# Sixteen-head local attention in f32: the product with V taken in two rounds of 64-row tiles, root steps kept in PSUM, and a new table of places

## The reference

```
for i in range(6):
    x = attn_layer(shift_tokens(x), Wqkv[i], q_scale[i], k_scale[i], Wo[i]) + x
    x = ffn_layer(shift_tokens(x), ln_g[i], ln_b[i], W1[i], b1[i], W2[i], b2[i]) + x

# attn_layer: 16 heads of 64; q, k normalised per head, rotated (rotary tables)
# local_attention, windows of w = 32 tokens:
bk2, bv2 = look(bk), look(bv)                 # window before, own window
sim = einsum('bhwie,bhwje->bhwij', bq, bk2) * 8
sim = where(mask, -max, sim)                  # of the 64 keys: 0 <= i - j <= 32
attn = softmax(sim, -1)
out = einsum('bhwij,bhwje->bhwie', attn, bv2)

# every normalisation: (x - mean) / sqrt(var + 1e-5)
```

## Time and profile before

| | before |
|---|---|
| median of 3 runs | 3553.56 us (3552.68 to 3554.56) |
| profiled execution, first to last instruction | 3553.3 us |
| TensorE matmul busy | 3325.9 us (94%) |
| VectorE busy | 2737.3 us (77%) |
| ScalarE busy | 2545.5 us (72%) |
| GpSimd busy | 2041.5 us (57%) |
| bytes moved by DMA | 423.34 MB, 119 GB/s |

### The profile page before, as it was taken

How to read it: one execution, slowest core, us unless ns; L and a number is a source line. 1 busy time by engine, 2 the same in 40 slices (tenths; PEclk the granted TensorE clock), 3 DMA queues, 4 the chain that set the end, 5 groups by cost and what they waited for, 6 DMA issues and landing times.

```text
span 3553.3 us, 149054 instructions
## 1 busy us (share of the span) xinstructions
PE 3325.9 (94%) x65032; PEld 2107.6 (59%) x65032; DVE 2737.3 (77%) x3420; ACT 2545.5 (72%) x5866; POOL 2041.5 (57%) x1557
## 2 busy tenths in 40 slices
PE   7999987999999999999999999999999999999996
PEld 3444434666666666666666666666666666666663
DVE  3656557888887878888788878788888878788883
ACT  4667655777777777777777767677777777787774
POOL 0000006766676666766666666667676667676661
PEclk9999998999999999999999999999999999999998
DMA  3223224333333333433333333334333333333330
GB/s 109 76 71 84 75 61 141 135 127 127 134 133 133 118 127 130 140 131 129 119 122 136 130 124 127 127 124 143 126 130 126 121 136 125 135 127 131 129 122 24
DMA packets 247337, 423.34 MB, mean 119 GB/s; under 512 B 71966, under 2 KB 110108, under 8 KB 246556
## 3 DMA queue, kind: packets, MB, share of 16 engines
q1 hardware_dynamic: 220368, 397.28, 33.1%
q10 hardware_dynamic: 26316, 16.52, 1.6%
HBM read 124.21 MB, written 7.34 MB: 37 GB/s over the span
## 4 chain that ended last, share of the span: by engine, by line
PE 64%; DVE 17%; issue 7%; ACT 5%; POOL 5%; DMA 1%; SPq 1%; DVEq 0%; POOLq 0%; ACTq 0%
PE PS L535 64%; DVE TPB L932 5%; DVE MX L956 2%; ACT SC L1237 1%; DVE NV L947 1%; POOL K L1324 1%; POOL Q L1342 1%; DMA RB<-root_scratch 1%; POOL K L1342 1%; DVE PP L977 1%; DVE PX L978 1%; DVE NV L945 1%; DVE H L800 1%; DVE H L1000 1%; DVE NV L949 1%
## 5 line engine op out<-in xcount | busy, mean ns | idle before, releaser
L932 DVE SCALAR_TENSOR_TENSOR TPB<-PS,VEC,C 128x1024 f32<-128x1024 f32 x768 | 961.8, 1270 | 102.0 <-ACT SX L1213 95.0
L1237 ACT ACTIVATE SC<-PS,BQ,RQ 128x64 f32<-128x64 f32 x3072 | 979.5, 436 | 40.7 <-DVE BQ L961 40.3
L1213 ACT ACTIVATE SX<-PS 128x512 f32<-128x512 f32 x768 | 461.5, 620 | 391.4 <-PE PS L535 388.4
L1324 POOL TENSOR_TENSOR K<-K,RB 128x512 f32<-128x512 f32 x384 | 497.2, 1295 | 283.1 <-DMA RB<-root_scratch 278.4
L1347 POOL TENSOR_TENSOR SC<-SC,RC 128x1024 f32<-128x1024 f32 x192 | 366.3, 1908 | 480.2 <-DVE RC L969 478.8
L535 PEld LDWEIGHTS PS<-PP,VV 32*64 32x64 f32 x24576 | 433.7, 133 | 278.6 <-issue 276.3
L535 PE MATMUL PS<-PP,VV 32*64 32x64 f32 (+1 forms) x24576 | 541.2, 223 | 7.8 <-issue 6.2
L1342 POOL TENSOR_TENSOR K<-TPB,TR 128x512 f32<-128x512 f32 x384 | 496.4, 1293 | 0.0
L1342 POOL TENSOR_TENSOR Q<-TPB,TR 128x512 f32<-128x512 f32 x384 | 495.5, 1290 | 0.0
L535 PE MATMUL PS<-LXH,LH 128*128 128x512 f32 x768 | 371.3, 484 | 85.2 <-DVE TPB L932 68.4
L535 PE MATMUL PS<-K,Q 64*32 64x64 f32 (+1 forms) x24576 | 302.2, 224 | 49.5 <-issue 48.0
(11 more groups left out here) (167 smaller groups left out, 5809.8 us busy)
## 6 DMA issues: line engine op xcount, KB each, us to landing
TR<-TPB SPq DMA_DIRECT2D x768, 256.0 KB, 2.7
RB<-root_scratch SPq DMA_DIRECT2D x768, 128.0 KB
PP<-PX SPq DMA_DIRECT2D x192, 192.0 KB, 2.6
WS<-in_wqkv ACTq DMA_DIRECT2D x72, 128.0 KB, 2.4
PP<-PX SPq DMA_DIRECT2D x192, 48.0 KB, 2.5
QA<-TH SPq DMA_DIRECT2D x128, 64.0 KB, 2.1
QA<-TL SPq DMA_DIRECT2D x128, 64.0 KB, 2.1
KA<-TH SPq DMA_DIRECT2D x128, 64.0 KB, 2.1
```

What stands on the lines that cost most here:

```text
L932: e.scalar_tensor_tensor(TPB[:, n % 3:4 + n % 2:3 + n % 2 - n % 3, w, :], g, VEC[:, l, 9 + w:10 + w], C[:, at:at + 1024].rearrange("p (o c ...
L1213: e.activation(SX[i % 3][:, :], bk("PJ", key)[:, :], ACT.Square).then_inc(sem["pj_act"], 1)
L1237: p = e.activation(SC[m % 2][:, g, :, :].rearrange("p x k -> p (x k)"), bank[s][:, at:at + 64], ACT.Exp, bias=BQ[m % 2][:, g:g + 1], scale ...
L1324: e.tensor_tensor(dst, dst, RB[n % 2][:, :], ALU.mult).then_inc(sem["pr_pool"], 1)
```

## The change

1. **PV in two rounds.** The keys of two windows stand together in one tile of K = 64 rows. Their queries span three windows, so the moving operand has 96 columns, and `PP` gets three blocks instead of two; where a key window is not used by a query window, the block is zero. A round still has 16 matmuls.
2. **Where the probabilities come from.** Both transposes write to staging tiles (`PX[0]`, `PX[1]`), and eight DMAs of 32 partitions carry them to their blocks. GpSimd zeroes `PP` once.
3. **Root steps in PSUM.** `rsqrt` writes its first two steps back into the bank, the third one too for F2, and F3 reads the bank. `FX` and `EZ` are gone. The F2 bank is now held until F3 is done, and the banks of the other normalisations until the third step.
4. **A new `PLACE`.** Nearly all numbers move a little. ScalarE has two table loads a unit, as before.

```diff
-    o.put("N2", kind, b, banks=[(None, kind + "_root", 3, 1)])
-    o.keep(o.bank["N2", (kind, b), 0], kind + "_root", 3 * b + 1)
+    o.put("N2", kind, b, banks=[(None, kind + "_root", 3, 3)])
+    o.keep(o.bank["N2", (kind, b), 0], kind + "_root", 3 * b + 3)
...
-        lay(z + P["F2"], group, "F2", u, "f2_dve", 3 * u + 1)
+        lay(z + P["F2"], group, "F2", u, "f3_dve", u + 1)
...
-                        on.wait_ge("pv_pe", 4 * m - 4)
-                    on.wait_ge("tt_dve", 2 * m + 2)
-                    e.dma_start(z[0:96, 1, :, :], a[32:128, :, :]).then_inc(sem[f"px_in{m % 2}"], 16)
-                    e.dma_start(z[96:128, 1, :, :].rearrange("p (x c) a -> p x c a", c=4)[:, :, 0:3, :],
-                                a[0:32, :, :].rearrange("p (x c) a -> p x c a", c=4)[:, :, 1:4, :]).then_inc(sem[f"px_in{m % 2}"], 16)
+                        on.wait_ge("pv_pe", 2 * m - 2)
+                    on.wait_ge("tt_dve", 2 * m + 1)
+                    for r in range(4):
+                        k = slice(32 * r, 32 * r + 32)
+                        e.dma_start(z[k, r % 2, :, :], PX[0][k, :, :]).then_inc(sem[f"px_in{m % 2}"], 16)
+                    on.wait_ge("tt_dve", 2 * m + 2)
+                    for r in range(1, 4):
+                        e.dma_start(z[32 * r - 32:32 * r, 1 + (r + 1) % 2, :, :],
+                                    PX[1][32 * r:32 * r + 32, :, :]).then_inc(sem[f"px_in{m % 2}"], 16)
+                    e.dma_start(z[96:128, 2, :, :].rearrange("p (x c) a -> p x c a", c=4)[:, :, 0:3, :],
+                                PX[1][0:32, :, :].rearrange("p (x c) a -> p x c a", c=4)[:, :, 1:4, :]).then_inc(sem[f"px_in{m % 2}"], 16)
...
                     for c in range(4):
-                        for x in range(2):
+                        for t in range(2):
                             for s in range(2):
-                                r = (rho + 2 * x + s) % 4
-                                j = 4 * c + r
-                                w = min(2, 16 - j)
+                                x = (t + rho) % 2
+                                j = 4 * c + 2 * t
+                                w = min(3, 16 - j)
                                 h = 2 * ((2 * p + x) % 8) + s
-                                y = mm(bank[2 + x][64 * s:64 * s + 64, 32 * j:32 * j + 32 * w],
-                                       VV[32 * r:32 * r + 32, c, 64 * h:64 * h + 64],
-                                       PP[p % 2][32 * r:32 * r + 32, 0:w, 8 * s + 4 * x + c, :],
-                                       rho == 0 and c == 0, rho == 3 and c == 3, skip_group_check=True)
+                                k = slice(64 * t, 64 * t + 64)
+                                y = mm(bank[2 + x][64 * s:64 * s + 64, 32 * j:32 * j + 32 * w], VV[k, c, 64 * h:64 * h + 64],
+                                       PP[p % 2][k, 0:w, 8 * s + 4 * x + c, :], rho == 0 and c == 0, rho == 1 and c == 3,
+                                       skip_group_check=True)
...
-            def rsqrt(v, u, x, step, done, r):
+            def rsqrt(v, x, y, step, done, r):
                 on.wait_ge(step, 2 * r + 2)
-                e.scalar_tensor_tensor(u, v, EPS, x, ALU.add, ALU.mult).then_inc(sem[done], 1)
+                e.scalar_tensor_tensor(v, v, EPS, x, ALU.add, ALU.mult).then_inc(sem[done], 1)
                 on.wait_ge(done, 3 * r + 1)
-                e.scalar_tensor_tensor(u, u, -0.5, x, ALU.mult, ALU.mult).then_inc(sem[done], 1)
+                e.scalar_tensor_tensor(v, v, -0.5, x, ALU.mult, ALU.mult).then_inc(sem[done], 1)
                 on.wait_ge(done, 3 * r + 2)
-                e.scalar_tensor_tensor(x, u, 1.5, x, ALU.add, ALU.mult).then_inc(sem[done], 1)
+                e.scalar_tensor_tensor(y, v, 1.5, x, ALU.add, ALU.mult).then_inc(sem[done], 1)
...
-                        on.wait_ge("pv_pe", 4 * m - 4)
                     on.wait_ge("np_pool", m + 1)
-                    e.transpose(PP[m % 2][:, 0, :, :], SC[m % 2][:, :, 1, :]).then_inc(sem["tt_dve"], 1)
-                    e.transpose(PX[:, :, :], SC[m % 2][:, :, 0, :]).then_inc(sem["tt_dve"], 1)
+                    e.transpose(PX[0][:, :, :], SC[m % 2][:, :, 1, :]).then_inc(sem["tt_dve"], 1)
+                    e.transpose(PX[1][:, :, :], SC[m % 2][:, :, 0, :]).then_inc(sem["tt_dve"], 1)
...
-                    rsqrt(bk("F2", key)[:, :], H[0][:, :], FX[:, :], "f2_act", "f2_dve", u)
+                    rsqrt(bk("F2", key)[:, :], H[0][:, :], bk("F2", key)[:, :], "f2_act", "f2_dve", u)
...
-                    e.tensor_tensor(H[2][:, :], H[1][:, :], FX[:, :], ALU.mult).then_inc(sem["f3_dve"], 1)
+                    e.tensor_tensor(H[2][:, :], H[1][:, :], bk("F2", key)[:, :], ALU.mult).then_inc(sem["f3_dve"], 1)
```

Of `PLACE`, the rows that the prediction speaks of:

```diff
-    ... "PV": (4.410, 5.233, 5.448, 5.789) ... "F2n": 14.625, "F3": 15.347 ... "NM2": -3.290, "RW": -3.234 ...
+    ... "PV": (4.497, 5.187) ... "F2n": 14.659, "F3": 14.692 ... "NM2": -3.084, "RW": -2.988 ...
```

More of the change, by code:

```diff
@@ L29 @@
 PLACE = {
[13 rows of a table removed]
[8 rows of a table added]
+    "AQd": -0.504, "AV": (-11.356, 0.560), "AVa": -0.483, "AS": -1.210, "ASa": -1.531, "ASd": -1.446, "AY": 0.834,
+    "AE": 2.282, "AEa": 3.137, "AR": (13.916, 25.437), "AI": (24.693, 25.209, 27.040), "AM": (28.617, 0.665),
+    "AMd": -0.785, "AO": (30.518, 0.702), "NM": (36.012, 37.027, 36.826), "AZ": 39.366,
+    "NX": (43.184, 43.848, 44.893), "AW": 47.832,
 }
@@ L294, in order @@
                 lay(n + P["S3"][i], o.put, "S3", m, i)
+            for i in range(2):
                 lay(n + P["PV"][i], o.put, "PV", m, i)
@@ L379, in build @@
         ES = sb("ES", [128, L])
-        EZ = sb("EZ", [128, L])
         SC = [sb(f"SC{i}", [128, 16, 2, 32]) for i in range(2)]
-        PP = [sb(f"PP{i}", [128, 2, 16, 32]) for i in range(2)]
-        PX = sb("PX", [128, 16, 32])
+        PP = [sb(f"PP{i}", [128, 3, 16, 32]) for i in range(2)]
+        PX = [sb(f"PX{i}", [128, 16, 32]) for i in range(2)]
         XCH = sb("XCH", [128, L], F32R)
@@ L427, in nroot @@
         def nroot(kind):
-            return EZ if kind == "end" else NZ[("in", "mid", "x").index(kind)]
+            return ES if kind == "end" else NZ[("in", "mid", "x").index(kind)]
         def nused(kind, b):
@@ L730, in tensor_program @@
                         on.wait_ge("vp_act", 8 * u + 4 * half + 4)
-                        on.wait_ge(f"px_in{p % 2}", 32 * (p // 2) + 32)
-                        on.wait_ge("tt_dve", 2 * p + 1)
+                        on.wait_ge(f"px_in{p % 2}", 128 * (p // 2) + 128)
                         if p:
@@ L832, in vector_program @@
                     kind, b = key
-                    rsqrt(bk("N2", key)[:, :], nsq(kind)[:, :], nroot(kind)[:, :], kind + "_log", kind + "_root", b)
+                    rsqrt(bk("N2", key)[:, :], nroot(kind)[:, :], nroot(kind)[:, :], kind + "_log", kind + "_root", b)
                 elif st == "AX":
@@ L1224, in scalar_program @@
                     if u:
-                        on.wait_ge("pv_pe", 16 * u - 8 + 8 * hf)
+                        on.wait_ge("pv_pe", 8 * u - 4 + 4 * hf)
                     on.wait_ge("vp_pe", j + 1)
@@ L1248, in scalar_program @@
                         on.wait_ge("wo_pe", p // 4)
-                    on.wait_ge("pv_pe", 4 * p + 4)
+                    on.wait_ge("pv_pe", 2 * p + 2)
                     e.copy(AOT[:, 2 * p % 8:2 * p % 8 + 2, :], PS[:, 2:4, :]).then_inc(sem["pv_act"], 1)
@@ L1263, in scalar_program @@
                     on.wait_ge("f2_pe", u + 1)
-                    ln_exp(H[0][:, :], bk(st, key)[:, :], FX[:, :], -0.5, "f2_act", u + 1, cn("hilo")[:, 3:4])
+                    ln_exp(H[0][:, :], bk(st, key)[:, :], H[0][:, :], -0.5, "f2_act", u + 1, cn("hilo")[:, 3:4])
                 elif st == "F4g":
@@ L1344, in gpsimd_program @@
                     m, = key
+                    if m == 0:
+                        for z in PP:
+                            e.memset(z[:, :, :, :], 0.0).then_inc(sem["band_pool"], 1)
                     on.wait_ge("su_dve", 2 * m + 2)
```

10 lines of the change are left out of this document (5 added, 5 removed), and 21 rows, old and new, of the table PLACE.

## The result

| | before | after |
|---|---|---|
| median | 3554.06 us (3552.68 to 3556.06) | 3614.09 us (3612.39 to 3616.03) |
| ratio, 95% interval | | 1.0171 [1.0156, 1.0185] |
| span of the profiled execution | 3553.3 us | 3613.1 us |
| granted clock over the span | 0.984 | 0.961 |
| bytes moved by DMA | 423.34 MB | 472.24 MB |

The change makes the kernel 60 us slower. The forecast was 3383 us with 0.93 for faster: wrong in sign, and 144 us above the top of the range.

What follows compares the result with a forecast made beforehand. TensorE was taken as the bound for some 70 to 77% of its busy time, VectorE for most of the rest. The sum was 3553.3 - 170 (rounds) - 12 (root steps) - 12 (stalls) + 24 (F2 bank) = 3383 us, range 3310 to 3470.

Steps and rivals of the forecast that it cites:

- the turn without queueing loads: TensorE's changed PV rounds: a turn takes 0.086 us, near its stream, bounds 0.080 and 0.113.
- TensorE's saving: PV in two rounds instead of four saves TensorE 1.14 us a pair, 219 us over 192 pairs.
- the stalls without a cause: TensorE's idle "issue" time, 44.4 us in the stretch: falls 19% with fewer records, 12 us gained.
- The rivals on loads: TensorE's PV rounds: loads queue within a row group (3446 us, chance 0.12) or never overlap its products (3662 us, 0.04).
- The prediction's sign of being wrong: GpSimd's wait for the norm roots' read-back well above its earlier share, TensorE waiting ahead of the scores; or rounds above 1.26 us.
- The table costed at nothing: New PLACE numbers: the shifted places leave the sequence around the costed points as it was, at no cost.
- the cover of 3.2 us: Time from GpSimd's end at 2050.30 to the scores' start at 2053.51, taken to hide roots' writes 2.0 us later.
- the case (3450 to 3550 us): Rival: SyncE's fuller queue and the F2 bank take the gain back, 3549 us at the worst; chance 0.08.
- The F2 bank term: TensorE's V projection waits for F3 on the held bank: 0.5 us a unit lost, 24 us, bounds 0 and 94.
- The share that reaches the end: Part of TensorE's 219 us that shortens the kernel: 0.775, products plus issue on the chain, giving 170 us.
- The rival in which all of it arrives: VectorE doesn't take over, so everything TensorE saves reaches the end: 3300 to 3330 us, chance 0.14.
- Root steps in PSUM: VectorE's three root steps take 646 ns each: 0.50 us a unit, 24 us, half on the chain, 12 gained.

Runs made afterwards that it cites:

- e4: Kernel before, with F2's root steps in PSUM, its bank held until F3, and F3 moved right behind the steps: 3662.34 us, ratio 1.0314.
- e6: Changed kernel with the table of before, F2's root steps in SBUF and its bank free after the first step: 3461.18 us, 0.9754 of before.
- e1: Changed kernel with the table of before, F3 right behind the third root step: 3515.32 us, 0.9904 of before.
- e5: Changed kernel with only the norm roots' two table numbers, NM2 and RW, set back to their old values: 3491.35 us, 0.9828 of before.
- e12: e4 plus twelve extra products, read by nobody, ahead of the projection that waits for F3: 3583.79 us, 1.0096 of before.
- e9: e6 with three DMAs a pair instead of eight, leaving out the placement of odd key windows: 3449.23 us, 0.9720 of before.
- e3: Changed kernel with F2's root steps in SBUF (third tile H[2]), its bank free after the first step: 3689.86 us, 1.0382 of before.

## Why the prediction was wrong

**Right:** the turn without queueing loads, the size of TensorE's saving (246 us; forecast 219), the root steps near 650 ns (696 to 699), a wait for F3 of about 2 us, and the direction of the stalls without a cause (44.4 us of 2000 before, 4.1 after, far more than the 19% forecast; in e4, with the old rounds, they are 47.5). The rivals on loads fell with the round of 0.81 us.

The 61 us divide so. Before to e6: -87, the rounds (with the eight DMAs and the other normalisations' steps in PSUM). e6 to e1: +53, F2's root in PSUM with its bank held, on the old table. e1 to after: +95, the new table. The forecast had -182 for the first (170 and 12 for the stalls), +12 for the second (24 less 12) and nothing for the third: 95, 41 and 95 us, which are the 231 between 3383 and 3614.

The prediction's sign of being wrong came as it was named: GpSimd waits 364.0 us for the roots against 181.2, and TensorE ahead of the scores.

**The table costed at nothing failed.** "The shifted places leave the sequence around these points as it was" was false of SyncE, where the order showed the writes moved behind the twin rows, as the prediction itself says; and it was false of VectorE, where the last steps on the norm roots moved behind another rotary product and, in every second group, behind L988. I had a price (2.0 us each, up to 192 us in all) and the cover of 3.2 us, and gave the case (3450 to 3550 us) 0.08, because 19 us of chain lie between the writes and the scores. The 2.0 counted SyncE's queue alone. What was measured, from the first step on the norm roots to the first write, is 8.2 us against 3.7, 4.5 us later. The 19 us are no slack: GpSimd and then TensorE do wait. The queue's part was near: the eight issues take 5.3 us a pair, not 4.8. e5 shows that two numbers of the table cost 122 us; the remaining ones gain 27 (e5 against e1).

**The F2 bank term was mis-sized.** It was 24 us, or 12 with the gain of the steps; e4 measures 112 with four rounds and e6 to e1 53 with two, both on the table of before. First, the product that waits was read wrongly. In the trace's names the moving operand stands first: `PS<-LXH,LH` is a Q or K projection and `PS<-LH,LXH` a V projection (514 of the first in the stretch and 256 of the second, Q and K against V); the description ahead of the prediction and the prediction itself have them the wrong way round. So what is late behind F3 is a Q/K projection, and with it its square and its rotary product, and not a V projection that nobody needs soon. "The long wait moves from the second place to the first, and 0.5 us a unit is lost" assumed that the second wait runs on untouched. e12 puts this part, less the gain of the steps, at 34 us; that the misread projection makes it is argued and not shown. Second, the clock: a gap of 2.21 us is followed by a stretch near 1.2 GHz, and this costs 77 us (e4 less e12). Before, the two waits of 0.57 and 1.60 us lay apart, and the clock was 0.99.

**The share that reaches the end failed.** 0.775 of 219 was 170 us. The rounds alone gain 87, or 99 with the queue's 12 of e9: 99 / 246 = 0.40. The shares of the chain before told what TensorE bounds at the old pace. After less than half of the saving VectorE and ScalarE are next (28.0% of the chain is TensorE's in e6). The rival in which all of it arrives fell too.

**Root steps in PSUM:** 12 us forecast. e3 gives 75 on the new table, but it also changes when the bank is free and shares `H[2]`. On the old table e6 and e1 differ by 53 the other way. No run changes only where the steps are written, so their own worth stays open.

## What to carry to other kernels

Count as moved whatever the order shows moved, on every engine that the data passes: a row behind one more rotary product or behind the twin rows is a change of its own, and its price has to be set against the whole chain behind it and not against the span of time until the last reader. Two waits brought together into one can cost more than their sum: in e4 TensorE's clock fell behind the longer one. Look at the granted clock right behind each gap, and test with idle work in the gap. The share of the chain that an engine has before a change says little of a large saving on it: here it was 0.70 to 0.775, and 0.40 arrived.
